# Two GNN layers on one core: receiver's term moved into message and table, deviation in halves, messages two chunks ahead, GpSimd's edge steps unrolled

## Chip and metric

The kernel runs on one core of a Trainium2 chip. The metric is the device time of one execution in microseconds. Median of three runs before the change: 1519.05 us (1518.92 to 1519.62).

## What is computed

x is 50000 nodes by 128 features. There are 25000 edges, sorted by receiver `dst`, each with a sender `src` and 128 attributes. Cut to what matters:

```python
def layer0(h, src, dst):                 # h = relu(layernorm(x))
    m = concat([h[dst], h[src]]) @ W_pre.T + b_pre
    mx, mn, mean, std = segment max, min, mean, sqrt(relu(E[m*m] - mean**2) + 1e-5) over dst
    agg = concat([mx, mn, mean, std])    # zero (std: sqrt(1e-5)) where a node has no edge
    amp = log(max(deg, 1) + 1)
    out = concat([h, agg, agg * amp, agg / amp]) @ W_post.T + b_post
    return out @ W_lin.T + b_lin
x = x + layer0(relu(layernorm(x)), src, dst)
h = relu(layernorm(x))
agg = segment mean of edge_attr over dst
x = x + relu(concat([h, agg]) @ W1 + b1) @ W2 + b2
```

## The kernel before

**Two phases.** The node phase walks over 98 chunks of 512 nodes and computes every node as if it had no edge: layer 0 reduces to a product with the combined weight `comb_x` and a constant, then the second layer norm and MLP, and the result goes to `out`. On its way it writes a table of 256 values a node to HBM: h = layernorm(x) and x. The edge phase walks over 49 chunks of 512 edges, gathers table rows by index (h of the sender into `hs`, h and x of the receiver into `rows`), computes both layers anew for nodes with edges, and scatters the results of each segment's last edge over `out`.

**Order of work.** Each engine runs its own program, written out by hand: `run_passes` calls `node_step(k)` and then `edge_step(k)`, and semaphores (`wait_ge`, `then_inc`) tie the engines together. In `edge_step(k)` an engine works on chunk k, on k+1 ("ahead") and on k-1 ("behind"). A function's first argument is the chunk. Instructions of an engine never overtake each other, nor do the DMAs of a queue in their issue.

**Matrix work of the edge phase** is on TensorE (`pe`). `sender_part` computes the senders' part of the messages of 512 edges by one float32 product; the receiver's term is the same for all edges of a segment and is added after the reduction. `layer0(c, j)` makes tile j of chunk c: for maximum, minimum and mean the value is split in a high and a low float32r half and multiplied in three passes of 384 columns (L607, L608, L611); the deviation is one float32 product (L614); the receiver's h, also split, has three more passes (L617). `hidden` (L699 to L703) and `outputs` are the second layer's MLP.

**VectorE (`dve`)** runs the segmented scans over the messages (`scan_max`, `scan_min`, `scan_sum`, `scan_squares`), the scan over the scaled attributes (`scan_attr`, L1219), `mix` (four tiles a chunk, three instructions each), the low halves (`low_part`), `factors` (L1191, L1193) and `outputs`. **ScalarE (`act`)** evicts, squares, makes the high halves, seeds the accumulators (`seed`), scales the attributes by 1/degree (`scale_attr`, L892) and makes the second layer norm's statistics (`squares`, L814; `spread`, L822) and `normalise`. **GpSimd (`pool`)** issues the indirect DMAs: eight gathers and four scatters a chunk; it copies their indices out of `index` first, and `factor` out of `scale`.

**SyncE (`sp`)** issues the plain DMAs. In `edge_step(k)` it loads five mask rows of chunk k+4 into four buffers, broadcast to 128 partitions, and then the attributes of chunk k+2 into two buffers. The masks' buffers are free when chunk k's scans have read them, so the first mask's DMA waits, among others, for `scan_attr(k)` (the first line quoted stands in the masks' part, where c is k+4):

```python
                        sp.wait_ge(sem("e_attr_run"), c - 3 + EU * i)
                    ...
                c = k + 2
                if edge(c):
                    ...
                        sp.wait_ge(sem("e_turned_attr"), c - 1 + EU * i)
```

The attributes' way is: SyncE's DMA, `scale_attr` on ScalarE, `turn_attr` on TensorE (a transpose into bank 2), `scan_attr` on VectorE.

## Time and profile before

| | us |
|---|---|
| median of three runs | 1519.05 |
| the profiled execution | 1520.14 |
| its span in the trace | 1518.3 |
| TensorE busy | 1445.0 |
| VectorE busy | 1287.0 |
| ScalarE busy | 1142.2 |
| GpSimd busy | 1152.0 |

Times in the trace are microseconds from the span's start. The node phase ends near 550 us, the edge phase's first `layer0` stands near 586 us. Busy time is the union of an engine's instructions; TensorE's instructions overlap each other, so that what one costs is read from start to start, and not from its duration.

### The profile page before, as it was taken

How to read it: one execution, taken by the hardware profiler on the slowest of the kernel's cores; microseconds unless marked ns; L12 is line 12 of the kernel's file. 1: busy time of each engine (PE TensorE's matmuls, PEld its weight loads, DVE VectorE, ACT ScalarE, POOL GpSimd, SP SyncE). 2: the span in 40 equal slices, each digit the busy share in tenths (PEclk: the TensorE clock that was granted, in tenths of full speed). 3: DMA queues.
4: the chain of work that ended last, by engine and by line, in shares of the span. 5: the costliest groups of instructions: out<-in, count | busy, mean ns of one | idle time of the engine just before them, and what ended most of it. 6: DMA issues, size and time to landing. Idle time of an engine off the chain costs nothing.

```text
span 1518.3 us, 34851 instructions
## 1 busy us (share of the span) xinstructions
PE 1445.0 (95%) x8704; PEld 1246.4 (82%) x8704; DVE 1287.0 (85%) x4128; ACT 1142.2 (75%) x2760; POOL 1152.0 (76%) x1427
## 2 busy tenths in 40 slices
PE   2799999999999987999999999999999999999994
PEld 2698998998998976888888888888888888888883
DVE  4899999999999957888888888888888888888881
ACT  1699999999999965777777777777777777777772
POOL 0677777777877876788888888888888888888722
PEclk9699999999999998999999999999999999999997
DMA  3455555555555563343434434333333443444200
GB/s 80 153 204 200 208 200 200 212 198 203 209 196 209 204 228 104 116 116 116 119 111 114 116 113 113 115 114 116 116 115 115 117 117 116 117 119 119 91 16 13
DMA packets 166068, 210.91 MB, mean 139 GB/s; under 512 B 19710, under 2 KB 116217, under 8 KB 166026
## 3 DMA queue, kind: packets, MB, share of 16 engines
q1 hardware_dynamic: 144074, 162.88, 32.7%
q0 software_dynamic: 21952, 47.55, 10.5%
q8 instruction: 17, 0.28, 0.1%
q14 instruction: 25, 0.20, 0.0%
HBM read 123.96 MB, written 90.27 MB: 141 GB/s over the span
## 4 chain that ended last, share of the span: by engine, by line
PE 92%; DVE 2%; issue 2%; DMA 1%; POOL 1%; ACT 1%; SPq 1%; DVEq 0%; POOLq 0%
PE bank L573 12%; PE bank L614 8%; PE bank L617 7%; PE bank L611 7%; PE bank L608 7%; PE bank L607 7%; PE bank L582 6%; PE bank L711 6%; PE bank L699 5%; PE bank L674 3%; PE bank L592 3%; PE bank L594 3%; PE bank L593 3%; PE bank L556 3%; PE bank L564 3%
## 5 line engine op out<-in xcount | busy, mean ns | idle before, releaser
L464 POOL DMA_INDIRECT y<-nout,oidx x196 | 223.3, 1139 | 49.0 <-issue 46.0
L456 POOL DMA_INDIRECT rows<-table,idx x196 | 187.9, 958 | 59.7 <-issue 59.7
L607 PE MATMUL bank<-comb_lo,agg_hi 128*128 128x384 f32 x588 | 221.3, 376 | 0.8 <-ACT bank L885 0.8
L456 POOL DMA_INDIRECT hs<-table,idx x196 | 192.8, 984 | 29.4 <-issue 10.0
L385 POOL TENSOR_TENSOR runs<-nx,b_all 128x512 f32<-128x512 f32 x98 | 125.5, 1281 | 114.6 <-DVE nx L1081 114.6
L573 PE MATMUL bank<-w_sb,nut 128*128 128x128 f32 x1568 | 202.0, 282 | 1.5 <-ACT nut L806 1.5
L573 PEld LDWEIGHTS bank<-w_sb,nut 128*128 128x128 f32 x1568 | 183.9, 193 | 19.8 <-issue 10.0
L611 PE MATMUL bank<-comb_hi,agg_lo 128*128 128x384 f32 x588 | 198.2, 337 | 0.0
L608 PE MATMUL bank<-comb_hi,agg_hi 128*128 128x384 f32 x588 | 198.1, 337 | 0.0
L791 ACT ACTIVATE nh<-nx,nms,nrs 128x128 f32<-128x128 f32 x392 | 161.8, 483 | 1.1 <-DVE nms L1054 0.5
L614 PE MATMUL bank<-comb_sd,agg_sd 128*128 128x384 f32 x392 | 158.1, 485 | 0.0
L397 POOL TENSOR_SCALAR rows<-rows,nmv,nrs 128x128 f32<-128x128 f32 x196 | 153.8, 794 | 0.0
L394 POOL TENSOR_TENSOR xdc<-rows,lone_const 128x512 f32<-128x512 f32 x98 | 124.7, 1272 | 34.4 <-DVE nrs L1091 34.4
L1147 DVE SCALAR_TENSOR_TENSOR part<-bank,factor,rows 128x128 f32<-128x128 f32 x196 | 67.9, 347 | 83.5 <-PE bank L617 83.4
L806 ACT ACTIVATE nut<-bank,b_col 128x512 f32<-128x512 f32 x196 | 126.3, 681 | 6.8 <-PE bank L594 6.6
L885 ACT ACTIVATE bank<-acc_seed 128x384 f32<-128x384 f32 x196 | 96.0, 490 | 43.0 <-DVE nx L1163 38.6
L876 ACT ACTIVATE nut<-bank,b_col 128x512 f32<-128x512 f32 x98 | 66.6, 680 | 79.2 <-PE bank L703 79.2
L617 PE MATMUL bank<-comb_h_lo,hdt 128*128 128x384 f32 x196 | 123.1, 628 | 0.0
L607 PEld LDWEIGHTS bank<-comb_lo,agg_hi 128*128 128x128 f32 x588 | 110.7, 188 | 14.8 <-ACT bank L885 10.7
L608 PEld LDWEIGHTS bank<-comb_hi,agg_hi 128*128 128x128 f32 x588 | 110.8, 188 | 13.5 <-issue 11.5
L611 PEld LDWEIGHTS bank<-comb_hi,agg_lo 128*128 128x128 f32 x588 | 110.5, 188 | 0.2 <-DVE agg_lo L1171 0.2
L582 PE MATMUL bank<-comb_x,hst 128*128 128x128 f32 x784 | 107.6, 282 | 2.8 <-ACT hst L770 2.8
(184 smaller groups left out, 4192.1 us busy)
## 6 DMA issues: line engine op xcount, KB each, us to landing
table<-rows SPq DMA_DIRECT2D x98, 512.0 KB, 2.7
rows<-in_x SPq DMA_DIRECT2D x98, 256.0 KB, 3.1
y<-nout SPq DMA_DIRECT2D x98, 256.0 KB, 2.7
inv<-inv_row SPq DMA_DIRECT2D x49, 256.0 KB, 5.0
keepm<-keepm_row SPq DMA_DIRECT2D x49, 256.0 KB, 5.8
attr<-in_edge_attr SPq DMA_DIRECT2D x48, 256.0 KB
keep<-keep_row SPq DMA_DIRECT2D x49, 128.0 KB, 3.6
reset<-reset_row SPq DMA_DIRECT2D x49, 128.0 KB, 4.6
```

Source lines behind the costliest of these rows:

```text
L397: last = pool.tensor_scalar(nh[:, c % 4, j, :], nx[:, c % 4, j, :], nmv1[:, c % 4, j, 0:1], nrs1[:, c % 4, j:j + 1], ALU.subtract, ALU.mult)
L456: pool.indirect_dma_start(out=to[:, s, j, :], out_offset=None, in_=of, in_offset=bass.IndirectOffsetOnAxis(ap=idx[:, s, which, j:j + 1], a ...
L464: pool.indirect_dma_start(out=out, out_offset=bass.IndirectOffsetOnAxis(ap=oidx[:, c % 4, j:j + 1], axis=0), in_=eout[:, c % 2, j, :], in_ ...
L573: mm = pe.matmul(bank[5][:, j * P:(j + 1) * P], nut[:, c % 2, m, j * P:(j + 1) * P], w2_sb[:, m, :], start=(m == 0), stop=(m == 1))
L582: mm = pe.matmul(bank[1][:, j * P:(j + 1) * P], nht[:, c % 2, j * P:(j + 1) * P], comb_x[:], start=True, stop=True)
L607: pe.matmul(acc[:, 0:SCALERS * P], hi, w_lo, start=False, stop=False, skip_group_check=True)
L608: pe.matmul(acc[:, 0:SCALERS * P], hi, w_hi, start=False, stop=False, skip_group_check=True)
L611: pe.matmul(acc[:, 0:SCALERS * P], lo, w_hi, start=False, stop=False, skip_group_check=True)
L614: pe.matmul(acc[:, 0:SCALERS * P], agg_sd[:, c % 2, cols], comb_sd[:].rearrange("p s f -> p (s f)"), start=False, stop=False, skip_group_c ...
L617: mm = pe.matmul(acc[:, 0:SCALERS * P], h[:, c % 2, cols], w[:].rearrange("p s f -> p (s f)"), start=False, stop=(w is comb_h_hi and h is ...
L791: last = act.activation(nh2[:, b, j, :], nx1[:, b, j, :], ACT.Identity, scale=nrs2[:, b, j:j + 1], bias=nms2[:, b, j:j + 1])
L806: act.activation(nut[:, c % 2, m, :], bank[6 + m][:], ACT.Relu, bias=b1_col[:, m:m + 1]).then_inc(sem("n_ut"), 1)
```

## The change

**Table and message.** `rows` now holds h and x1, x1 being the node's value after the first layer as if it had no edge (the node phase's `nx1`); x itself has a tile of its own, `nx`. The table is written in step k for chunk k, after `n_x1`, where it was chunk k+2. The edge phase starts from x1, and the accumulator's seed leaves out what x1 holds already. The receiver's term goes into the message: `messages` is `sender_part` with a second float32 product of 512 columns (`wd_t`, `hdt`); the three passes with `comb_h_lo` and `comb_h_hi`, and VectorE's `receiver_low`, are gone. **Deviation.** It is split into halves like the other three aggregates, with three float32r passes for one float32 product, a `high_part` on ScalarE and a `low_part` on VectorE. **Order.** Messages are made for chunk k+2 in step k, and all engines' edge steps are put in another order. **GpSimd.** No index copies, its edge steps written out for every chunk, one small operation (`go`) ahead of each four DMAs; `copy_factors` moves to VectorE. SyncE's `edge_step` is as it was.

The diff, cut to its core:

```diff
-    nh, nx = rows[:, :, :, 0:P], rows[:, :, :, P:2 * P]
-    hd, xd = nh, nx
+    nh, nx1 = rows[:, :, :, 0:P], rows[:, :, :, P:2 * P]
+    hd, xd = nh, nx1
+    nx = sb("nx", [P, 4, TILES, P])
...
-                        sp.wait_ge(sem(f"n_tabled{c % 4}"), 16 * (c // 4) + 16 * i)
-                        sp.wait_ge(sem("n_turn1"), c - 3 + NU * i)
+                        sp.wait_ge(sem("n_norm1"), c - 3 + NU * i)
+                        sp.wait_ge(sem("n_norm1_act"), c - 3 + NU * i)
+                        sp.wait_ge(sem("n_norm1_pool"), c - 3 + NU * i)
                         sp.wait_ge(sem("n_xc"), c - 3 + NU * i)
                     sp.dma_start(nx[:, c % 4], node_rows(x, c, i)).then_inc(sem(f"n_in{c % 4}"), 16)
-                c = k + 2
+                c = k
                 if node(c):
 
                     sp.wait_ge(sem("n_norm1"), c + 1 + NU * i)
                     sp.wait_ge(sem("n_norm1_act"), c + 1 + NU * i)
                     sp.wait_ge(sem("n_norm1_pool"), c + 1 + NU * i)
+                    sp.wait_ge(sem("n_x1"), c + 1 + NU * i)
...
+                    pool.wait_ge(sem(f"e_gathered{s}"), 16 * 2 * TILES * (c // 4))
+                    pool.wait_ge(sem("e_turned_s"), c - 3)
+                    pool.wait_ge(sem("e_turned_d"), c - 3)
+                go(0, c, "e_mixed" if c >= 4 else None, TILES * (c - 3))
+                gather_tile(c, 0)
+                gather_tile(c, 1)
+                go(1, c, None, 0)
+                gather_tile(c, 2)
+                gather_tile(c, 3)
...
+                go(2, c, "e_out", c + 1)
                 for j in range(TILES):
-                    if j == 2:
-                        pause(2, c, i)
                     pool.indirect_dma_start(
-                        out=out, out_offset=bass.IndirectOffsetOnAxis(ap=oidx[:, c % 4, j:j + 1], axis=0),
+                        out=out, out_offset=bass.IndirectOffsetOnAxis(ap=column(2, c, j), axis=0),
                         in_=eout[:, c % 2, j, :], in_offset=None,
                         bounds_check=N - 1, oob_is_err=False).then_inc(sem(f"e_scattered{c % 4}"), 16)
...
-                for a in (MX, MN, ME):
+                for a in (MX, MN, ME, SD):
...
-                pe.matmul(acc[:, 0:SCALERS * P], agg_sd[:, c % 2, cols], comb_sd[:].rearrange("p s f -> p (s f)"),
-                          start=False, stop=False, skip_group_check=True)
-                for h, w in ((hdt, comb_h_lo), (hdl, comb_h_hi), (hdt, comb_h_hi)):
-                    mm = pe.matmul(acc[:, 0:SCALERS * P], h[:, c % 2, cols], w[:].rearrange("p s f -> p (s f)"),
-                                   start=False, stop=(w is comb_h_hi and h is hdt), skip_group_check=True)
+                    mm = pe.matmul(acc[:, 0:SCALERS * P], lo, w_hi, start=False, stop=(a == SD), skip_group_check=True)
...
-                pe.matmul(bank[3 + c % 2][:], ws_t[:], hst[:, c % 2, :], start=True, stop=True).then_inc(sem("e_b_psum"), 1)
+                pe.matmul(bank[3 + c % 2][:], ws_t[:], hst[:, c % 2, :], start=True, stop=False)
+                pe.wait_ge(sem("e_hdt"), c + 1 + EU * i)
+                pe.matmul(bank[3 + c % 2][:], wd_t[:], hdt[:, c % 2, :], start=False, stop=True).then_inc(sem("e_b_psum"), 1)
...
-                if ahead:
-                    turn_sender(k + 1, i)
-                    turn_receiver(k + 1, i)
                 if have:
                     turn_attr(k, i)
-                if ahead:
-                    sender_part(k + 1, i)
+                if edge(k + 2):
+                    turn_sender(k + 2, i)
+                    turn_receiver(k + 2, i)
                 if have:
-                    pe.wait_ge(sem("e_hdl"), k + 1 + EU * i)
                     layer0(k, 0, i)
                     layer0(k, 1, i)
+                if edge(k + 2):
+                    messages(k + 2, i)
                 if behind:
-                    turn_normed(k - 1, i, not ahead)
+                    turn_normed(k - 1, i, not edge(k + 2))
...
             def edge_step(k, i):
                 have, ahead, behind = edge(k), edge(k + 1), edge(k - 1)
                 if k == 0:
                     seed(0, 0, i)
                 if ahead:
-                    sender_turned(k + 1, i)
+                    scale_attr(k + 1, i)
+                if behind:
+                    squares(k - 1, i)
                 if have:
                     seed(k, 1, i)
                 if behind:
-                    squares(k - 1, i)
                     spread(k - 1, i)
-                if ahead:
-                    message_squared(k + 1, i)
+                if edge(k + 2):
+                    receiver_turned(k + 2, i)
+                    sender_turned(k + 2, i)
                 if behind:
                     normalise(k - 1, i)
                 if have:
                     seed(k, 2, i)
+                if ahead:
+                    mean_squared(k + 1, i)
                 if behind:
                     normed_turned(k - 1, i)
                 if ahead:
-                    receiver_turned(k + 1, i)
-                    scale_attr(k + 1, i)
                     high_part(ME, "e_mean_b", mean_b[:], k + 1, i)
+                    high_part(MX, "e_max", run_max[:, (k + 1) % 2, :], k + 1, i)
+                    variance_pos(k + 1, i)
+                    high_part(MN, "e_min", run_min[:, (k + 1) % 2, :], k + 1, i)
+                    deviation(k + 1, i)
                 if behind:
                     hidden(0, 7, k - 1, i)
                 if have:
                     seed(k, 3, i)
                 if ahead:
-                    mean_squared(k + 1, i)
+                    high_part(SD, "e_std", var[:], k + 1, i)
                 if behind:
                     out_bias(k - 1, i)
-                if ahead:
-                    high_part(MN, "e_min", run_min[:, (k + 1) % 2, :], k + 1, i)
+                if edge(k + 2):
+                    message_squared(k + 2, i)
                 if behind:
                     hidden(1, 1, k - 1, i)
                 if ahead:
                     if k >= 0:
                         seed(k + 1, 0, i)
-                    variance_pos(k + 1, i)
-                    deviation(k + 1, i)
-                    high_part(MX, "e_max", run_max[:, (k + 1) % 2, :], k + 1, i)
...
@@ -1299,41 +1281,41 @@
 
             def edge_step(k, i):
                 have, ahead, behind = edge(k), edge(k + 1), edge(k - 1)
-                if have:
-                    scan_attr(k, i)
+                if ahead:
+                    scan_max(k + 1, i)
+                    scan_squares(k + 1, i)
+                    scan_sum(k + 1, i)
                 if edge(k - 2):
                     outputs(k - 2, i)
                 if behind:
                     factors(k - 1, i)
+                if ahead:
+                    message_mean(k + 1, i)
                 if have:
                     mix(k, 0, i)
                 if ahead:
-                    scan_sum(k + 1, i)
+                    square_mean(k + 1, i)
                     scan_min(k + 1, i)
-                    message_mean(k + 1, i)
+                    variance(k + 1, i)
                 if behind:
                     normed_low(k - 1, i)
-                if ahead:
-                    receiver_low(k + 1, i)
                 if have:
                     mix(k, 1, i)
                 if ahead:
-                    scan_squares(k + 1, i)
+                    low_part(MX, run_max[:, (k + 1) % 2, :], k + 1, i)
+                if have:
+                    scan_attr(k, i)
+                    mix(k, 2, i)
+                if edge(k + 2):
+                    copy_factors(k + 2, i)
+                if ahead:
+                    low_part(MN, run_min[:, (k + 1) % 2, :], k + 1, i)
                     low_part(ME, mean_b[:], k + 1, i)
-                    square_mean(k + 1, i)
-                if have:
-                    mix(k, 2, i)
-                if ahead:
-                    variance(k + 1, i)
-                    scan_max(k + 1, i)
                 if have:
                     mix(k, 3, i)
-                if ahead:
-                    low_part(MN, run_min[:, (k + 1) % 2, :], k + 1, i)
-                if have:
                     negative_mean(k, i)
                 if ahead:
-                    low_part(MX, run_max[:, (k + 1) % 2, :], k + 1, i)
+                    low_part(SD, var[:], k + 1, i)
 
             run_passes(dve, node_step, edge_step, first_step=-1)
 
```

Three places in the order of instructions. On VectorE, one edge step of the loop around `scan_attr`; before it was the first work of the step (`runs<-keepm` is `scan_attr`, `part` and `nx` are `mix`):

```order
L1219 SCALAR_TENSOR_TENSOR runs<-keepm,runs,bank 128x512 [waits e_u_psum]
L1183 TENSOR_TENSOR nout<-bank,nx 128x512 [waits e_scattered0]
L1191 RECIPROCAL rs<-sd 128x4 [waits e_norm2]
L1193 SCALAR_TENSOR_TENSOR ms<-neg,rs 128x4 [waits e_rs2]
L1147 SCALAR_TENSOR_TENSOR part<-bank,factor,rows 128x128 [waits e_factors,e_gathered0]
L1153 SCALAR_TENSOR_TENSOR part<-bank,factor,part 128x128 [waits e_part]
L1163 SCALAR_TENSOR_TENSOR nx,sum<-bank,part 128x128 [waits e_ms2,e_norm2,e_part2]
L1257 SCALAR_TENSOR_TENSOR runs<-keep,runs,bank 128x512 [waits e_sum,e_mean_b,e_masks_in1,e_bsq]
```

and with the change, from `factors` to `scan_attr` of one step:

```order
L1178 RECIPROCAL rs<-sd 128x4 [waits e_norm2]
L1180 SCALAR_TENSOR_TENSOR ms<-neg,rs 128x4 [waits e_rs2]
L1257 TENSOR_TENSOR mean_b<-runs,inv 128x512 [waits e_mean_b2,e_lo2,e_sum]
L1130 SCALAR_TENSOR_TENSOR part<-bank,factor,rows 128x128 [waits e_factors,e_gathered0]
L1136 SCALAR_TENSOR_TENSOR part<-bank,factor,part 128x128 [waits e_part]
L1150 SCALAR_TENSOR_TENSOR nx,sum<-bank,part 128x128 [waits e_ms2,e_norm2,e_part2]
...
L1228 SCALAR_TENSOR_TENSOR runs<-lift,runs,bank 128x512 [waits e_min,e_lo1,e_masks_in1,e_bsq]
L1270 TENSOR_TENSOR var<-var,mean_b 128x512 [waits e_sq_mean,e_mean_b2]
L1187 SCALAR_TENSOR_TENSOR nh2l<-bank,nh2t 128x512 [waits e_u_psum]
...
L1158 TENSOR_TENSOR agg_lo<-runs,agg_hi 128x512 [waits e_layer0]
L1200 SCALAR_TENSOR_TENSOR runs<-keepm,runs,bank 128x512 [waits e_u_psum]
```

`scan_attr(k)` has moved from ahead of `factors(k-1)` (`rs<-sd`, `ms<-neg,rs`) to behind `factors(k-1)`, two mixes, a scan and five elementwise operations.

On ScalarE, before, the end of one step and the start of the next (`attr<-attr,factor` is `scale_attr`, `sq<-nx,neg` is `squares`, `sd<-sq` is `spread`):

```order
L892 ACTIVATE attr<-attr,factor 128x128 [waits e_factors,e_attr_in0]
L892 ACTIVATE attr<-attr,factor 128x128 x3
...
L885 ACTIVATE bank<-acc_seed 128x384 [waits e_mixed]
L814 ACTIVATE off,sq<-nx,neg 128x128 [waits e_sq2,e_neg2]
L814 ACTIVATE off,sq<-nx,neg 128x128 x3
L822 ACTIVATE sd<-sq,eps_col 128x4 [waits e_rs2,e_sq2]
L852 ACTIVATE bsq<-bank 128x512 [waits e_sqsum,e_b_psum]
```

and with the change, the start of a step:

```order
L863 ACTIVATE attr<-attr,factor 128x128 [waits e_factors,e_attr_in0]
L863 ACTIVATE attr<-attr,factor 128x128 x3
L785 ACTIVATE nx,sq<-nx,neg 128x128 [waits e_sq2,e_neg2]
L785 ACTIVATE nx,sq<-nx,neg 128x128 x3
L856 ACTIVATE bank<-acc_seed 128x384 [waits e_mixed]
L793 ACTIVATE sd<-sq,eps_col 128x4 [waits e_rs2,e_sq2]
```

`scale_attr(k+1)` stood in step k behind `squares(k-1)` and `spread(k-1)`, and now stands ahead of both.

On SyncE, the issues of one step with the change; the list before reads the same but for the line numbers:

```order
L340 DMA keep<-keep_row 128x512 [waits e_sq_mean,e_mean_b,e_attr_run,e_min,e_max]
L340 DMA reset<-reset_row 128x512
L340 DMA lift<-lift_row 128x512
L340 DMA inv<-inv_row 128x512
L340 DMA keepm<-keepm_row 128x512
L352 DMA attr<-in_edge_attr 128x4x128 [waits e_turned_attr]
```

Nothing moved there: the attributes' DMA is queued behind five masks, whose first waits for `e_attr_run`, which `scan_attr` raises.

## Rows read from the trace of the kernel before

**Rows 1.** One stretch: busy PE, PEld, DVE, ACT, POOL; then PEclk, DMA share, GB/s

```profile
800.00:1100.00 300.00, 300.00 (x1620) 253.64 (x1619) 254.02 (x534) 220.65 (x551) 250.26 (x340) 1.00 0.40 115
```

**Rows 2.** Timeline of TensorE over one edge step (start, duration, us)

```profile
844.85 0.81 PE L614 MATMUL bank<-comb_sd,agg_sd 128*128 128x384 f32 x2
...
845.84 0.34 PE L617 MATMUL bank<-comb_h_hi,hdt 128*128 128x384 f32 x1
846.01 0.34 PE L607 MATMUL bank<-comb_lo,agg_hi 128*128 128x384 f32 x1
...
851.94 1.02 PE L699 MATMUL bank<-runs,w_attr 128*128 128x512 f32 x2
...
853.49 1.02 PE L699 MATMUL bank<-runs,w_attr 128*128 128x512 f32 x2
...
863.39 0.81 PE L614 MATMUL bank<-comb_sd,agg_sd 128*128 128x384 f32 x2
```

**Rows 3.** Timeline of VectorE over the same step

```profile
842.68 1.28 DVE L1219 TENSOR_TENSOR_SCAN runs<-keepm,runs,bank 128x512 f32<-128x512 f32 x1 [0.83 <-issue]
...
844.56 0.18 DVE L1191 RECIPROCAL rs<-sd 128x4 f32<-128x4 f32 x1
844.77 0.16 DVE L1193 SCALAR_TENSOR_TENSOR ms<-neg,rs 128x4 f32<-128x4 f32 x1
846.21 0.35 DVE L1147 SCALAR_TENSOR_TENSOR part<-bank,factor,rows 128x128 f32<-128x128 f32 x1 [1.27 <-PE bank L617]
...
847.25 1.28 DVE L1257 TENSOR_TENSOR_SCAN runs<-keep,runs,bank 128x512 f32<-128x512 bf16 x1
848.45 1.25 DVE L1247 TENSOR_TENSOR_SCAN runs<-lift,runs,bank 128x512 f32<-128x512 bf16 x1
849.62 0.67 DVE L1276 TENSOR_TENSOR mean_b<-runs,inv 128x512 f32<-128x512 f32 x1
850.20 0.68 DVE L1206 SCALAR_TENSOR_TENSOR nh2l<-bank,nh2t 128x512 fp32r<-128x512 f32 x1
```

**Rows 4.** Timeline of ScalarE over the same step

```profile
842.15 0.49 ACT L885 ACTIVATE bank<-acc_seed 128x384 f32<-128x384 f32 x1
...
844.23 0.30 ACT L822 ACTIVATE sd<-sq,eps_col 128x4 f32<-128x4 f32 x1
...
850.35 1.27 ACT L892 ACTIVATE attr<-attr,factor 128x128 f32<-128x128 f32 x4
```

**Rows 5.** Timeline of SyncE's DMA issues in the same step

```profile
844.18 0.33 SPq L341 DMA_DIRECT2D keep<-keep_row  x1
...
846.08 0.38 SPq L341 DMA_DIRECT2D keepm<-keepm_row  x1
846.65 0.38 SPq L353 DMA_DIRECT2D attr<-in_edge_attr  x1
```

**Rows 6.** The tile keep, 600 to 1430 us: issue to landing

```profile
DMA to landing us min/median/max: 3.2/3.6/4.2
```

**Rows 7.** The tile keepm, 600 to 1430 us: issue to landing

```profile
DMA to landing us min/median/max: 4.8/5.8/6.4
```

**Rows 8.** GpSimd's DMA groups on the page

```profile
L464 POOL DMA_INDIRECT y<-nout,oidx x196 | 223.3, 1139 | 49.0 <-issue 46.0
L456 POOL DMA_INDIRECT rows<-table,idx x196 | 187.9, 958 | 59.7 <-issue 59.7
...
L456 POOL DMA_INDIRECT hs<-table,idx x196 | 192.8, 984 | 29.4 <-issue 10.0
```

**Rows 9.** Timeline of VectorE, then of GpSimd, near 611 us

```profile
611.30 1.28 DVE L1267 TENSOR_TENSOR_SCAN runs<-keep,runs,bsq 128x512 f32<-128x512 bf16 x1
...
611.67 1.66 POOL L456 DMA_INDIRECT rows<-table,idx  x1 [0.30 <-issue]
```

**Rows 10.** Timelines at the change of phase: GpSimd, then TensorE

```profile
549.56 1.22 POOL L456 DMA_INDIRECT hs<-table,idx  x1 [0.17 <-issue]
...
552.38 0.60 PE L564 MATMUL bank<-ident,nh 128*128 128x128 f32 x4
```

More of the change, by code:

```diff
@@ L236, in run_passes @@
                 edge_step(k - N_HI + 1, 0)
+        if not edge_loop:
+            for k in range(0, E_HI):
+                edge_step(k, 0)
+            return
         for k in range(0, E_LOOP):
@@ L692, in hidden @@
                     pe.wait_ge(sem("e_out"), c + EU * i)
-                if m == 1 and edge(c + 2):
-                    pe.wait_ge(sem("e_hdl"), c + 3 + EU * i)
+                if m == 1 and edge(c + 3):
+                    pe.wait_ge(sem("e_hdt"), c + 4 + EU * i)
                 if c >= 1:
```

202 lines of the change are left out of this document (86 added, 116 removed).

## The prediction, made blind

> **What bounds the kernel now.** I read first the busy time by stretch. Between 800 and 1100 us TensorE is busy for all 300 us at a granted clock of 1.00 (its upper level, 2.4 GHz), while VectorE has 254, GpSimd 250 and ScalarE 221 [rows 1]. So in the edge phase nothing but TensorE's own instructions sets the pace, and every other wait has slack. The period of a chunk is read from one instruction to the same one a step later: the deviation's product of the same tile starts at 844.85 and again at 863.39, so 18.54 us a chunk [rows 2]; 49 chunks make about 908 of the 1518.3 us. The node phase before it is no place where the change moves much: its work a chunk is the same, only the table's write moves by two steps.
>
> **TensorE's part.** From the deviation's product to the next tile's first pass it is 846.01 − 844.85 = 1.16 us a tile: one float32 product and three receiver passes. One float32r pass of 384 columns costs 846.01 − 845.84 = 0.17 [rows 2]. In their place stand three float32r passes, 0.52. That removes 0.64 a tile, 2.56 a chunk. Added is a float32 product of 512 columns. From one such product of the MLP to the next is 853.49 − 851.94 = 1.55, with three float32r products of 512 between; at 0.17 × 512/384 = 0.23 each the float32 one costs 0.86. Net −1.70: TensorE needs **16.84 us a chunk**.
>
> **The other engines.** VectorE loses a low half (`receiver_low`) and gains one (deviation) of 0.58, the step from 849.62 to 850.20 [rows 3], and the factors' copy, taken at 0.2, near the smallest operation there (0.18): about 254/300 × 18.54 = 15.7, and with the small gaps between operations some 16.3. ScalarE: 221/300 × 18.54 = 13.6, and the new high half about as much as a low half, 14.2. GpSimd issues 12 DMAs a chunk: (223.3 + 187.9 + 192.8)/49 = 12.33 [rows 8], with 0.30 of gap ahead of one [rows 9], nine such gaps 2.7. The three `go` are new and no row shows them: at least one small operation (0.18, VectorE's in rows 3, for want of one of GpSimd's), at most a DMA's gap and such an operation, 0.5; I take 0.5 since each waits for semaphores. 12.33 + 2.7 + 1.5 = 16.5. The index copies, 250/300 × 18.54 − 12.33 = 3.1 of today's busy time, go. So all engines together would allow about 17.
>
> **The wait that takes their place.** It is a loop through four engines, one step a turn, and I went round it because the change moves two of its members. Before, `scan_attr(k)` was the step's first work on VectorE; SyncE's first mask DMA followed it by 844.18 − (842.68 + 1.28) = 0.22 [rows 3, 5]; `scale_attr` of the attributes fetched then stood in the middle of ScalarE's next step. A ScalarE instruction at 850.35 [rows 4] used attributes whose DMA had been issued in the previous step; those issued at 846.65 [rows 5], landing near 852 by the estimate below, are used at 850.35 + 18.54 = 868.9. That is 17 us of slack, nearly a step.
>
> After, `scan_attr(k)` stands behind `factors(k-1)`, two mixes and a scan, and `scale_attr(k+2)` is the very first work of ScalarE's step k+1, ahead of `squares(k)` and `spread(k)`, on which `factors(k)` and so `scan_attr(k+1)` depend. The turn of the loop is:
> - scan's end to the first mask's issue: 0.22.
> - to the attributes' landing: their DMA is the sixth in the queue. The fifth, `keepm`, is issued 846.08 − 844.18 = 1.90 after the first [rows 5] and lands 5.8 later in the median [rows 7], so at 7.7; the attributes are issued 0.57 later. Nothing waits for them in the trace of before, so their landing is not shown. I take 7.95, between 7.7 (with `keepm`) and 8.27 (0.57 later), since each mask lands later than the one ahead of it: the first takes 3.6 [rows 6].
> - ScalarE: `scale_attr` 1.27, then `squares` with one seed 844.23 − 842.15 = 2.08, then `spread` 0.30 [rows 4]: 3.65.
> - VectorE: `factors` 844.77 − 844.56 + 0.16 = 0.37; five operations of 0.58 (mean, square mean, variance, `normed_low`, low half), 2.90; two mixes of 847.25 − 846.21 = 1.04, 2.08; `scan_min` 849.62 − 848.45 = 1.17; `scan_attr` 1.28 [rows 3]: 7.80.
>
> Sum 0.22 + 7.95 + 3.65 + 7.80 = **19.6 us a chunk**. This is more than 18.54, and no engine's work lies beside it: while ScalarE waits for the attributes, everything behind in its queue waits too (`squares`, seeds, the receiver's and sender's copies), so TensorE's `layer0` of tile 1 and on waits for seeds, and VectorE's mixes for TensorE. What is late next would be the masks themselves, which have two steps.
>
> Bounds of the unknown landing: the quickest `keepm` (4.8) puts it at 1.90 + 4.8 = 6.7 and the loop at 18.4 (1509); landing as an unloaded mask does, 1.90 + 0.57 + 3.2 [rows 5, 6] = 5.7, puts it at 17.35; the slowest `keepm` plus 0.57, 8.9, at 20.55.
>
> The Trainium skill ("DMA: Bandwidth & Descriptors", section "Queues, rings and completion order") says that a ring's descriptors are consumed in ring order. The rows bear on it: the fifth mask lands 5.8 after its issue and the first 3.6, though the same size [rows 6, 7]; by that rule the attributes land behind `keepm`, as taken above.
>
> **The phase's start and end.** The first messages now need gathers of chunk 2 as well, and the table's last chunk is complete only with the node phase's x1: the first gather, at 549.56 now, comes at about 552, when TensorE turns the last node chunk's normed rows [rows 10], +2.4; partly covered. I take +1.5, between 0 (hidden in the 36 us to the first `layer0`) and 3. In the last three steps no masks are issued ahead of the attributes or no attributes at all: these run at TensorE's 16.84, 3 × (16.84 − 18.54) = −5.1.
>
> **The sum**, against the profiled execution: 1520.1 + 45 × (19.6 − 18.54) + 1.5 − 5.1 = 1564.2. That execution was 1.1 above the median of the runs, so **1563**. In general the time is 1515.4 + 45 × (T − 18.54) with T the period, and it equals 1519 at T = 18.62. The measurement tells about 0.2% (3 us) from no change.
>
> **Rivals.**
> - *TensorE still sets the pace*, and the time falls: T = 16.84 gives 1439. For it: TensorE was at 300 of 300 [rows 1]. Against: the loop, and GpSimd at about the same length. It needs the attributes to land within 16.84 − 11.67 = 5.2 of the scan's end, less than any row gives.
> - *GpSimd sets the pace.* A gather that begins while VectorE runs a scan with two operands in SBUF is stretched until that scan ends: 1.66 instead of its mean 0.958 at 611.67, the scan ending at 611.30 + 1.28 = 612.58 [rows 8, 9]. With DMAs back to back, one or two more in a chunk meet this: 16.5 + about 0.8 = 17.3, time 1460. It decides if the attributes land before 17.3 − 11.67 = 5.6. The Trainium skill ("SBUF — State Buffer", section "Who interferes with whom") says that a VectorE instruction with two SBUF inputs contends with GpSimd's; the trace agrees in these rows.
> - *The loop exists but the DMAs land sooner*, since the queue is less crowded when VectorE is idle: T between 17.35 and 18.6, time 1462 to 1518. For it: the minima in rows 6 and 7. Against: the masks' five broadcasts go together whatever VectorE does, and the median of `keepm` is 1 us over its minimum.
> - *The loop is worse*: the landing of 8.9 gives 20.55 and 1606; and GpSimd's gathers, now packed in fours, share the DMA engines.
>
> **Chances.** Loop over 18.7: 0.71 (its own range 1530 to 1606); loop between 18.55 and 18.7, a time within 3 us: 0.04; loop below: 0.09; GpSimd: 0.09; TensorE: 0.07. Faster thus 0.25, same 0.04, slower 0.71. For 8 in 10 the range runs from 1462, the loop's low bound and just above GpSimd's time, to 1604, near the high bound; outside lie TensorE's and most of GpSimd's case (0.14) and a worse loop (0.05).
>
> **What would show it.** Right: in the edge phase the same product of a tile comes each 19.6 us; TensorE's busy time there falls to some 16.8/19.6 of it, with the idle time before tiles that wait for seeds or mixes; ScalarE sits idle for about 5 us a chunk before `scale_attr`, released by the attributes' DMA; VectorE's `factors` waits for `spread`; SyncE's first mask waits for `scan_attr`. A DMA landing row for the attributes of 5 to 6 us settles the largest term. Wrong, and the time near 1440 to 1460, if the attributes land within 3 us of their issue; then ScalarE's wait is gone and TensorE or GpSimd is busy throughout. Wrong the other way, if a mix or a seed waits for GpSimd's gathers or scatters, which I cost at nothing since rows and factors are gathered two steps ahead.

## The result, and the profile after

The changed kernel took **1657.89 us** in the median of four runs (1650.22 to 1669.53) against 1519.09 for the kernel before beside it: ratio 1.092, 95% interval 1.085 to 1.099. I had forecast 1563 with a range of 1462 to 1604. The direction was right and the loop that I had named is there; but one wait in it was left out, the size was off by 95 us, and the range did not hold the time.

One caution for all that follows: in three groups of runs the kernel before took 1645 to 1772 us, and times from those groups are told apart below and never set against 1519 or 1658.

The page of the profiled execution (1655.76 us) says in its first rows what changed: the span, the busy time of TensorE, and the chain of work that ended last, traced back from the last instruction. TensorE made 92% of that chain before; now it makes 48%.

```profile
span 1653.9 us, 34363 instructions
...
PE 1431.4 (87%) x8403; PEld 1241.9 (75%) x8403; DVE 1291.1 (78%) x4180; ACT 1152.0 (70%) x2812; POOL 1104.8 (67%) x1134
...
PE 48%; DMA 16%; issue 10%; ACT 9%; DVE 8%; SPq 6%; POOL 2%; DVEq 0%; ACTq 0%; POOLq 0%
DMA attr<-in_edge_attr 15%; PE bank L542 11%; SPq L340 6%; PE bank L551 5%; ACT nx L785 4%; PE bank L576 4%; DVE runs L1200 3%; PE bank L636 3%; PE bank L577 3%; PE bank L580 3%; PE bank L561 3%; PE bank L563 3%; PE bank L562 3%; PE bank L525 3%; PE bank L533 3%
```

The same row of the kernel before:

```profile
PE 92%; DVE 2%; issue 2%; DMA 1%; POOL 1%; ACT 1%; SPq 1%; DVEq 0%; POOLq 0%
```

The DMA of the attributes is now the costliest member of the chain, 15% of the span. The busy times by stretch have the columns of [rows 1]. First the node phase of the kernel before, then two stretches of the changed kernel. The node phase is as before, and between 800 and 1100 us no engine is full any more.

```profile
200.00:400.00 200.00, 200.00 (x1477) 180.32 (x1475) 196.54 (x972) 184.85 (x428) 157.65 (x157) 1.00 0.56 203
```

```profile
200.00:400.00 200.00, 200.00 (x1476) 180.74 (x1474) 196.10 (x972) 186.40 (x428) 157.77 (x157) 1.00 0.57 203
800.00:1100.00 300.00, 257.56 (x1285) 220.28 (x1284) 215.66 (x467) 187.10 (x481) 198.43 (x206) 0.89 0.34 99
```

TensorE has 257.6 of 300 at a mean granted clock of 0.89 where it had 300 at 1.00. The cost per chunk is read from one `negative_mean` (`neg<-sum`, near the end of VectorE's step) to the next. The first, the 46th and the last of the changed kernel, and then of the kernel before:

```profile
604.96 0.17 DVE L1280 TENSOR_SCALAR neg<-sum 128x4 f32<-128x4 f32 x1
...
1577.64 0.17 DVE L1280 TENSOR_SCALAR neg<-sum 128x4 f32<-128x4 f32 x1
...
1624.58 0.17 DVE L1280 TENSOR_SCALAR neg<-sum 128x4 f32<-128x4 f32 x1
```

```profile
601.17 0.16 DVE L1298 TENSOR_SCALAR neg<-sum 128x4 f32<-128x4 f32 x1
...
1435.10 0.33 DVE L1298 TENSOR_SCALAR neg<-sum 128x4 f32<-128x4 f32 x1
...
1488.59 0.17 DVE L1298 TENSOR_SCALAR neg<-sum 128x4 f32<-128x4 f32 x1
```

The first 45 periods take 1577.64 − 604.96 = 972.7, **21.6 us a chunk** (18.53 before, 18.54 in [rows 2]); the last three take 46.9 together. The whole difference of the two profiled executions, 135.6 us, is 138.7 in these 45 periods, 3.8 in the start of the phase, −6.5 in the last three chunks and −0.4 in the tail.

**The loop, once round.** The chain of waits, from one `scan_attr` (L1200) to the next (start, duration; a name and a line for each piece):

```profile
1018.70 1.28 DVE runs L1200
1020.20 0.33 SPq L340
1020.62 0.38 SPq L340
1021.10 0.38 SPq L340
1021.66 0.33 SPq L340
1022.09 0.38 SPq L340
1022.65 5.34 DMA attr<-in_edge_attr
1028.10 0.14 ACT attr L863
...
1029.38 1.54 ACT nx L785 x8
1030.91 0.39 ACT bank L856
1031.34 0.44 PE bank L576
...
1034.95 0.30 PE bank L580
1035.26 0.86 PE bank L636 x2
1036.12 0.86 PE bank L638 x2
1036.97 0.45 PE bank L648 x4
1037.53 0.61 ACT nh2t L829
1038.27 0.06 DVE nh2l L1187
...
1040.47 1.28 DVE runs L1200
```

It is the forecast loop: the scan, five masks (L340), the attributes' DMA, `scale_attr` (L863), `squares` (L785). But from there the chain does not go over `spread` and `factors` to VectorE. It goes over `seed(k,1)` (L856) to TensorE: `layer0` of tile 1, twelve passes, then `messages` (L636, L638), `turn_normed` (L648), back to ScalarE (`nh2t`) and only then to VectorE's `normed_low` (L1187). ScalarE's and VectorE's timelines show the same as waits (the bracket is idle time before the row, and who ended it):

```profile
1028.10 1.28 ACT L863 ACTIVATE attr<-attr,factor 128x128 f32<-128x128 f32 x4 [5.00 <-DMA attr<-in_edge_attr]
...
1031.23 0.28 ACT L793 ACTIVATE sd<-sq,eps_col 128x4 f32<-128x4 f32 x1
...
1037.53 0.60 ACT L829 ACTIVATE nh2t<-bank 128x512 fp32r<-128x512 f32 x1 [2.58 <-PE bank L648]
```

```profile
1031.63 0.18 DVE L1178 RECIPROCAL rs<-sd 128x4 f32<-128x4 f32 x1 [2.29 <-ACT sd L793]
...
1038.27 0.69 DVE L1187 SCALAR_TENSOR_TENSOR nh2l<-bank,nh2t 128x512 fp32r<-128x512 f32 x1 [2.26 <-ACT nh2t L829]
```

ScalarE waits 5.00 us for the attributes, as forecast ("about 5 us"). VectorE waits 2.29 for `spread`, as forecast, and then once more, 2.26, for `nh2t`, which was not. The attributes' landing over the phase (issue to landing):

```profile
DMA to landing us min/median/max: 3.9/5.5/6.6
```

Five and a half in the median. With 1.90 + 0.57 = 2.47 from the first mask to the issue of the attributes, that makes 7.97. The turn's terms, mean of the first 42 turns in the trace (each read from rows like those above), beside the forecast:

| term | forecast | measured |
|---|---|---|
| scan's end to first mask | 0.22 | 0.23 |
| to the attributes' landing | 7.95 | 7.97 |
| ScalarE: `scale_attr`, `squares`, seed, `spread` | 3.65 | 3.41 |
| to `factors` | 0 | 0.06 |
| VectorE's own work, `factors` to scan's end | 7.80 | 7.86 |
| VectorE's wait for `nh2t` | 0 | 2.00 |
| turn | 19.6 | 21.5 |

**The wait has three sizes**, and they go with TensorE's clock in tile 1 and in the messages behind it. "Tile 1" is the time from its first pass to the first product of the messages; the 42 turns are those of the table above:

| turns | granted clock in tile 1 | tile 1 | messages | wait for `nh2t` | turn |
|---|---|---|---|---|---|
| 13 | 1.00 | 2.2 | 1.7 | 0.59 to 0.73, mean 0.65 | 20.2 |
| 17 | 0.54 to 0.76 | 2.8 to 3.8 | 1.7 to 2.8 | 1.81 to 2.35, mean 2.11 | 21.5 |
| 12 | 0.50 | 4.0 | 2.3 to 2.8 | 2.68 to 3.48, mean 3.27 | 23.1 |

The turn shown above is one of the 17. TensorE had stood idle for 3.02 us before tile 1, and most of its passes then follow each other at 0.32 instead of 0.17. Two windows, one in the work ahead of the idle time and one over tile 1, show the granted clock (the third number from the end):

```profile
1026.00:1028.00 2.00, 2.00 (x15) 2.00 (x12) 2.00 (x3) 0.00 (x0) 1.70 (x2) 1.00 0.66 213
1031.40:1035.00 3.60, 3.60 (x12) 3.60 (x13) 3.26 (x9) 3.55 (x9) 2.99 (x3) 0.54 0.31 91
```

The clock is 1.00 in the first, its upper level of 2.4 GHz. The mean of 0.54 in the second says that nearly all of it ran at the lower level of 1.2 GHz. Twelve passes that need 2.1 us took 3.7. In another turn TensorE came out of 3.16 us of idle time at the upper level; TensorE's timeline, and VectorE's behind it:

```profile
790.67 0.44 PE L576 MATMUL bank<-comb_lo,agg_hi 128*128 128x384 f32 x1 [3.16 <-ACT bank L856]
790.95 0.33 PE L577 MATMUL bank<-comb_hi,agg_hi 128*128 128x384 f32 x1
...
792.68 0.34 PE L580 MATMUL bank<-comb_hi,agg_lo 128*128 128x384 f32 x1
792.85 1.02 PE L636 MATMUL bank<-hst,ws_t 128*128 128x512 f32 x2
```

```profile
795.91 0.69 DVE L1187 SCALAR_TENSOR_TENSOR nh2l<-bank,nh2t 128x512 fp32r<-128x512 f32 x1 [0.67 <-ACT nh2t L829]
```

The tile takes 792.85 − 790.67 = 2.18, and VectorE waits 0.67. The idle time before tile 1 does not tell which it will be: it was 2.60 to 3.56 us before the 13 tiles at 1.00, and 2.34 to 5.91 before the other 29. The Trainium skill ("TensorE: Matmul & The Clock Gate", section "HAM oscillation — how this bites in real kernels") describes a kernel in which every DMA wait lowers the clock for the work behind it; the trace agrees for 29 of these 42 turns and not for the other 13, though every one of them has the wait for the attributes' DMA in it.

### The profile page after: what moved, and what is told of

It reads as the page before. It is cut to its first block, busy times and chain, and to the rows that moved or that the text cites. A ratio compares the mean times of both kernels' runs of the same rounds, so it can differ in the third digit from the quotient of the medians.

```text
span 1653.9 us, 34363 instructions
## 1 busy us (share of the span) xinstructions
PE 1431.4 (87%) x8403; PEld 1241.9 (75%) x8403; DVE 1291.1 (78%) x4180; ACT 1152.0 (70%) x2812; POOL 1104.8 (67%) x1134
## 4 chain that ended last, share of the span: by engine, by line
PE 48%; DMA 16%; issue 10%; ACT 9%; DVE 8%; SPq 6%; POOL 2%; DVEq 0%; ACTq 0%; POOLq 0%
DMA attr<-in_edge_attr 15%; PE bank L542 11%; SPq L340 6%; PE bank L551 5%; ACT nx L785 4%; PE bank L576 4%; DVE runs L1200 3%; PE bank L636 3%; PE bank L577 3%; PE bank L580 3%; PE bank L561 3%; PE bank L563 3%; PE bank L562 3%; PE bank L525 3%; PE bank L533 3%
## 5 line engine op out<-in xcount | busy, mean ns | idle before, releaser
L580 PE MATMUL bank<-comb_hi,agg_lo 128*128 128x384 f32 x784 | 284.2, 362 | 0.0
L577 PE MATMUL bank<-comb_hi,agg_hi 128*128 128x384 f32 x784 | 284.0, 362 | 0.0
L417 POOL DMA_INDIRECT rows<-table,index x196 | 242.8, 1239 | 60.8 <-issue 60.8
L451 POOL DMA_INDIRECT y<-nout,index x196 | 211.4, 1079 | 54.5 <-issue 54.3
L417 POOL DMA_INDIRECT hs<-table,index x196 | 199.7, 1019 | 45.2 <-issue 38.3
L863 ACT ACTIVATE attr<-attr,factor 128x128 f32<-128x128 f32 x196 | 62.6, 390 | 231.8 <-DMA attr<-in_edge_attr 231.8
L384 POOL TENSOR_TENSOR runs<-rows,b_all 128x512 f32<-128x512 f32 x98 | 126.0, 1285 | 113.0 <-DVE rows L1057 113.0
L755 ACT ACTIVATE nh<-rows,nms,nrs 128x128 f32<-128x128 f32 x392 | 161.8, 483 | 0.9 <-DVE nms L1030 0.3
L400 POOL TENSOR_SCALAR rows<-nx,nmv,nrs 128x128 f32<-128x128 f32 x196 | 154.6, 798 | 0.0
L397 POOL TENSOR_TENSOR xdc<-nx,lone_const 128x512 f32<-128x512 f32 x98 | 124.9, 1274 | 35.2 <-DVE nrs L1067 35.1
L1187 DVE SCALAR_TENSOR_TENSOR nh2l<-bank,nh2t 128x512 fp32r<-128x512 f32 x49 | 33.9, 691 | 97.8 <-ACT nh2t L829 97.8
L663 PE MATMUL bank<-runs,w_attr 128*128 128x512 f32 x196 | 101.9, 602 | 0.7 <-issue 0.7
```

The lines of the kernel that those rows point to most:

```text
L384: pool.tensor_tensor(nx1b[:, c % 4], nx1[:, c % 4], b2_all[:], ALU.add).then_inc(sem("n_x1b"), 1)
L397: pool.tensor_tensor(nxc[:, c % 2], nx[:, c % 4], lone_const[:], ALU.add).then_inc(sem("n_xc"), 1)
L400: last = pool.tensor_scalar(nh[:, c % 4, j, :], nx[:, c % 4, j, :], nmv1[:, c % 4, j, 0:1], nrs1[:, c % 4, j:j + 1], ALU.subtract, ALU.mult)
L417: pool.indirect_dma_start(out=to[:, s, j, :], out_offset=None, in_=of, in_offset=bass.IndirectOffsetOnAxis(ap=column(which, c, j), axis=0) ...
L451: pool.indirect_dma_start(out=out, out_offset=bass.IndirectOffsetOnAxis(ap=column(2, c, j), axis=0), in_=eout[:, c % 2, j, :], in_offset=None,
L577: pe.matmul(acc[:, 0:SCALERS * P], hi, w_hi, start=False, stop=False, skip_group_check=True)
```

## Experiments

### The attributes ahead of the masks

SyncE issues `attr(k+2)` before the masks of chunk k+4; its own wait (`turn_attr(k)`) is met early. The rest is the changed kernel.

```diff
             def edge_step(k, i):
+                c = k + 2
+                if edge(c):
+                    ...
+                        sp.dma_start(attr[:, s], ...)
                 c = k + 4
                 if edge(c):
                     ...
-                c = k + 2
-                ...
```

> The changed kernel with SyncE's attributes ahead of the masks, a third time, as the yardstick beside the two runs below. Theory: 2% below the kernel before on this chip, undisturbed chunks 16.4 to 17.8, stalls in the others.

Measured: **1459.21 us** (1456.80 to 1466.25), the kernel before 1519.06 beside it, ratio 0.962 (0.960 to 0.965). ScalarE no longer waits for the attributes at all. The loop alone had turned a gain of 60 us into a loss of 139. Of the first 45 periods 25 are 16.7 and 17 are 17.6 to 18.6; the mean is 17.2. What bounds it now is between TensorE and GpSimd. The stretch has the columns of [rows 1]; below it stand GpSimd's groups on the page:

```profile
800.00:1100.00 300.00, 293.56 (x1636) 252.27 (x1635) 273.18 (x594) 244.00 (x607) 243.16 (x264) 1.00 0.43 124
```

```profile
L417 POOL DMA_INDIRECT hs<-table,index x196 | 222.7, 1136 | 45.2 <-issue 42.1
L451 POOL DMA_INDIRECT y<-nout,index x196 | 212.3, 1083 | 54.5 <-issue 51.9
L417 POOL DMA_INDIRECT rows<-table,index x196 | 205.3, 1047 | 59.7 <-issue 59.7
```

GpSimd's DMAs cost (222.7 + 212.3 + 205.3)/49 = 13.07 a chunk instead of the 12.33 taken from [rows 8]; 85 of them follow each other from 849 to 970 us with at most 0.7 us between the end of one and the start of the next. This is the rival "GpSimd sets the pace", forecast at 17.3 and 1460; the two runs that follow bear on it.

### Fewer scatters

The same with three of a chunk's four scatters left out: those rows of the output are not written. The waits for the scatters count one a chunk instead of four.

```diff
-                for j in range(TILES):
+                for j in range(1):
                     pool.indirect_dma_start(
                         out=out, ...
```

> The kernel of attr_ahead with three of a chunk's four scatters left out, so that GpSimd issues 9 DMAs a chunk and rests some 4 us in each. Theory: the stalls come with GpSimd's unbroken series of DMAs (24 in a row, the stall in the last third), so they are gone: chunks of 16.4 to 17.4 throughout, time 1430 to 1470 on any chip. Rival: the stalls are the chip's or the other engines' own and stay: within 40 us of attr_ahead.

Measured: **1432.54 us** (1430.25 to 1435.37), ratio 0.943 (0.941 to 0.945), beside the 1459 above.

```profile
800.00:1100.00 300.00, 300.00 (x1691) 260.08 (x1690) 280.87 (x613) 250.72 (x630) 204.67 (x216) 1.00 0.41 121
```

TensorE is full, every period of the loop but the first is 16.7 (forecast 16.84), and GpSimd is busy for 205 of 300 us. So the three scatters cost 1459 − 1433 = 27 us of the version with the loop cut. The stalls that the expectation speaks of are told of below; attr_ahead had none of them beside this run, so the run can't say what ends them.

### GpSimd's program as before

The kernel of attr_ahead with the old `edge_step` of GpSimd: in a loop, with index copies and a small operation behind each two DMAs (the old `gather_rows_of`, `scatter_rows_of`, `go`, `pause`, `gather`, `scatter`; `copy_factors` stays on VectorE).

```diff
...
+                pool.tensor_copy(idx[:, s].rearrange("p w (r h) -> p w r h", h=2), index[:, 0:2, t, :]).then_inc(sem("e_idx"), 1)
...
+                    if j % 2 == 1:
+                        pause(j // 2, c, i)
...
-            run_passes(pool, node_step, edge_step, edge_loop=False)
+            run_passes(pool, node_step, edge_step)
```

> The kernel of attr_ahead with GpSimd's edge steps as before the change (in a loop, index copies, a small operation after each two DMAs). Theory: with its small operations GpSimd needs about 17.5 us a chunk and is as unbroken as before, so that the stalls stay as in attr_ahead, within 40 us of it. Rival, it is the unrolled GpSimd program or its missing pauses that stall the others: the stalls go, 1460 to 1500.

Measured: **1506.24 us** (1503.64 to 1511.22), ratio 0.991 (0.989 to 0.993). Neither expectation holds: it is 47 us over attr_ahead and 6 over the rival's range, at 16.7 to 22.9 a chunk. TensorE now waits for gathers that land late; the row of the table of waits between 660 and 1380 us that names them (us in total, times, longest):

```profile
PE bank L622 <- DMA rows<-table,idx: 45.6, 28, 3.4
```

So the new GpSimd program is worth 47 us once the loop is cut; which part of it, the unrolling, the missing small operations or the place of the waits, is not told apart.

### scale_attr back in the middle of ScalarE's step

```diff
-                if ahead:
-                    scale_attr(k + 1, i)
                 if behind:
                     squares(k - 1, i)
...
                     normed_turned(k - 1, i)
                 if ahead:
+                    scale_attr(k + 1, i)
                     high_part(ME, "e_mean_b", mean_b[:], k + 1, i)
```

> scale_attr(k+1) behind normed_turned(k-1) on ScalarE, SyncE as in the changed kernel. Theory: where the kernel before takes 1519 the loop is cut as in attr_ahead (1459) and GpSimd sets the pace: period 17.1 to 17.5, time 1455 to 1475. Rival: stalls of this order's own, as in the three runs where the kernel before took over 1640: over 1490 here too.

Measured: **1466.30 us** (1463.91 to 1468.34), the kernel before 1518.50, ratio 0.966 (0.964 to 0.967); of the first 45 periods all but the first are 17.3 to 17.5. Moving one call on ScalarE is enough to take away the whole loss. Nothing waits for the attributes' DMA, with SyncE's queue as it was. The period is GpSimd's: from 729 to 1387 us its 455 DMAs follow each other with at most 0.7 us between them, and twelve take 17.34 from start to start.

### turn_normed ahead of messages on TensorE

```diff
-                if edge(k + 2):
-                    messages(k + 2, i)
                 if behind:
                     turn_normed(k - 1, i, not edge(k + 2))
+                if edge(k + 2):
+                    messages(k + 2, i)
```

> turn_normed(k-1) ahead of messages(k+2) on TensorE, else the changed kernel. Theory: where the kernel before takes 1519, VectorE's wait for nh2t falls from 2.0 to under 0.4 us a chunk, the period from 21.5 to 19.6 to 19.9, the time from 1658 to 1575 to 1590. Rival: the time stays within 20 us of 1658 as another wait takes the place.

Measured: **1584.63 us** (1583.69 to 1585.86), the kernel before 1519.27, ratio 1.043 (1.041 to 1.045). The loop stays, its branch over TensorE gets shorter by the messages' 1.7 us. VectorE's wait for `nh2t` is 0.15 in the mean of the first 42 turns and zero in 27 of them; here one that has it:

```profile
1016.74 0.69 DVE L1187 SCALAR_TENSOR_TENSOR nh2l<-bank,nh2t 128x512 fp32r<-128x512 f32 x1 [0.54 <-ACT nh2t L829]
```

The mean turn in the trace is 20.0 (19.6 to 19.9 expected): the attributes land 8.31 after the first mask's issue here, instead of 7.97. This is very nearly the forecast's own loop, without the branch that it left out, and the time is 22 us over the forecast's 1563.

### Place in the queue or the wait

The attributes ahead of the masks, but still held until `scan_attr(k)`:

```diff
+                        sp.wait_ge(sem("e_turned_attr"), c - 1 + EU * i)
+                        sp.wait_ge(sem("e_attr_run"), c - 1 + EU * i)
+                    ...
+                        sp.dma_start(attr[:, s], ...)
                 c = k + 4
```

> The changed kernel with SyncE's DMA of the attributes of chunk k+2 ahead of the five masks' DMAs of chunk k+4 instead of behind them, still held until scan_attr(k) is done. It tells place in the queue from the wait. Theory: the loop holds, but 4.4 us of its 7.9 us from the scan's end to the landing are the queue; alone the attributes land in about 3.5 us as the first mask does; the period falls to about 17.1 or to what another engine allows, the time to 1450 to 1475. Rival, the transfer itself takes the 5.5 us from issue to landing that it shows now: only 2.5 us are saved, the period is 19.0 to 19.3 and the time 1540 to 1560.

> Attributes ahead of the masks in SyncE's queue but still held until scan_attr(k), where the kernel before takes 1519. Theory: the queue is 4.4 of the 7.9 us to the landing; period 17.1 to 17.5, time 1460 to 1480. Rival, the transfer itself takes 5.5 us: 19.0 to 19.3, 1540 to 1560.

Both runs fell where the kernel before took 1764 and 1772 us, so the times decide nothing on the forecast periods (1688.81, ratio 0.960, 0.952 to 0.968; 1681.10, ratio 0.944, 0.933 to 0.954; the changed kernel beside the second took 1710). The trace of the first shows one issue and the ScalarE instruction that waited for its landing:

```profile
752.95 0.38 SPq L335 DMA_DIRECT2D attr<-in_edge_attr  x1
...
755.92 1.28 ACT L864 ACTIVATE attr<-attr,factor 128x128 f32<-128x128 f32 x4 [0.54 <-DMA attr<-in_edge_attr]
```

It is 2.97 us from issue to use, where it takes 5.5 behind five masks. In the 26 turns of this trace in which ScalarE waited for the landing it is 2.5 to 3.0, in the 27 of the second 2.7 to 3.5. With the 2.47 of the five issues, 5.0 of the 8.0 us from the first mask's issue to the landing are the place behind the masks. That the period would fall to 17.1 is not shown.

### The same variants where the kernel before took 1645 to 1772 us

Three groups of runs, told apart by the second column. The first two were made before the runs above that have 1519 beside them, the third between those and the last two (scale_mid_d, turn_first_d). `after_again` is the changed kernel unaltered; the first group has no run of it:

| kernel | the kernel before beside it | time | ratio (95%) |
|---|---|---|---|
| turn_first | 1764 | 1655 | 0.939 (0.933 to 0.945) |
| scale_mid | 1764 | 1742 | none given |
| attr_ahead | 1764 | 1690 | 0.951 (0.942 to 0.960) |
| after_again | 1645 | 1697 | 1.037 (1.028 to 1.047) |
| turn_first_b | 1645 | 1654 | 1.006 (1.001 to 1.012) |
| scale_mid_b | 1645 | 1706 | 1.041 (1.032 to 1.050) |
| attr_ahead_b | 1645 | 1603 | 0.980 (0.971 to 0.990) |
| turn_first_c | 1772 | 1663 | 0.941 (0.933 to 0.948) |
| scale_mid_c | 1772 | 1755 | 0.989 (0.979 to 1.000) |
| after_again_c | 1772 | 1710 | 0.969 (0.963 to 0.976) |

> The changed kernel with one swap on TensorE: turn_normed(k-1) ahead of messages(k+2). Theory: the turn of the loop (attributes' DMA, scale_attr, squares, factors, scan_attr) has a side branch that I left out, seed(k,1), layer0(k,1) at the lower clock, messages(k+2), turn_normed, nh2t, normed_low, and it is this branch that VectorE waits for, 2.3 us a chunk. Without the messages' 1.7 us in it the period falls from 21.5 to about 19.8 and the time from 1658 by about 46 x 1.7 to 1575 to 1590. Rival: the branch is late because of something ahead of layer0 tile 1 alone, and the order behind it doesn't matter: 1640 to 1658.

> The changed kernel with scale_attr(k+1) on ScalarE moved from the front of the step to behind normed_turned(k-1), about where it was before the change. Theory: the DMA's latency lies beside ScalarE's work again, the loop is cut, TensorE or GpSimd sets the pace: period 16.9 to 17.4, time 1445 to 1470, no idle time of ScalarE ahead of scale_attr. Rival: the attributes are late for this place too, or other waits of the new order bound it: period 18 or more, time over 1495.

> The changed kernel with SyncE's DMA of the attributes of chunk k+2 ahead of the masks' and with only its own wait (turn_attr(k)), which is met at the start of TensorE's step k. Theory: the loop is cut at SyncE; the attributes have more than half a step to land; the period is that of TensorE or GpSimd, 16.9 to 17.4, time 1445 to 1470, the same as with scale_attr moved. Rival: if the place of scale_attr at the front of the step hurts by itself (it delays squares and factors by 1.3 us), this is slower than the kernel with scale_attr moved by 5 us or more.

> The changed kernel unaltered, beside the same variants on one chip. On the chip of the last four runs the kernel before took 1764 us instead of 1519, with waits that end at no instruction of the trace, so that those four can't be set against 1658. Theory: ratio to the kernel before 1.09 where that takes 1519; near 0.95 to 1.0 on a chip where it takes 1764. All comparisons of the variants are made with this run.

The b and c runs had much the same expectations. For turn_first_b it was 70 to 80 us below the changed kernel beside it, and for after_again_c a ratio of 1.09. Both missed. Against the changed kernel of its own group turn_first is 42 and 47 us lower, attr_ahead_b 94 lower, and scale_mid 9 and 45 higher. From these groups alone one would say that moving `scale_attr` does not help. The traces say otherwise: in scale_mid_b chunks of 16.7 to 17.8 alternate with chunks of 20 to 32, and in the long ones engines stand idle with all their inputs done. TensorE's timeline has the receiver's transposes, and ScalarE's the copy (L807) that waits for them and for nothing newer:

```profile
881.37 0.60 PE L615 MATMUL bank<-ident,rows 128*128 128x128 f32 x4
...
882.22 0.28 ACT L793 ACTIVATE sd<-sq,eps_col 128x4 f32<-128x4 f32 x1
890.33 0.60 ACT L807 ACTIVATE hdt<-bank 128x512 f32<-128x512 f32 x1 [7.83 <-remote]
```

The transposes end at 882.0 and ScalarE starts at 890.33, after 7.83 us that the profile puts down to no instruction of this core. I then supposed that GpSimd's unbroken series of DMAs (24 in a row, the stall in the last third) caused them, and expected that for the run with fewer scatters. An unbroken series alone does not do it: attr_ahead_c has 85 in a row and scale_mid_d 455, neither has such a stall, and in the group of attr_ahead_c the kernel before, run once more unaltered, has none either:

> The kernel before, for its trace on this chip: two chips have timed it at 1764 and 1645 us where the trace that I read had 1519. Theory: its edge phase has the same sort of stall as the variants with the loop cut (engines that stand idle for 3 to 12 us with every input done, late in a long unbroken series of GpSimd's DMAs), 120 to 245 us in all, and its undisturbed chunks still take 18.5. Rival: everything is uniformly slower, by a lower clock.

Measured: 1519.06 us (1517.41 to 1521.22), ratio 1.000, periods of 18.5 and 18.6 in all but the first and last of the edge phase. Neither the theory nor the rival could show, since the kernel before took 1519 here; no trace of it was taken where it took 1645 us or more. The group at 1645 and this one ran on the same chip, so it is not the chip alone; what makes the difference is open. In the traces of the slower groups the node phase is as in the others up to 540 us, and all that is longer stands behind it.

## Why the prediction missed

**What bounds before: right.** TensorE alone at 18.54.

**TensorE's new price: right.** 16.84 forecast, 16.7 measured where nothing else bounds (cut_few_scatters).

**GpSimd: the base too low, the rival right in its number.** 16.5 was the sum; the rival with stretched gathers said 17.3 and 1460; the kernel with the loop cut has 17.2 and 1459 (17.3 and 1466 in scale_mid_d). The DMAs rose from 12.33 to 13.07 a chunk. Its reason, gathers stretched by scans, holds in part. Between 620 and 1400 us 68 of 532 DMAs last over 1.4 us in attr_ahead_c, where it was 5 of 504 before; but only 18 of the 68 lie beside a scan, the others beside mixes, `normed_low` and other elementwise work of VectorE. The row that the rival was read from says less than was read: that gather ended at 611.67 + 1.66 = 613.33, which is 0.75 after the scan's end and not with it.

**The loop: found, and each term that was in its sum sized within 0.25 us.** scale_mid_d and attr_ahead_c, which each cut it at another place, both take its whole price away (192 and 199 us off 1658). The landing rested on a comparison that is not clean: the prediction calls `keep` and `keepm` the same size, and they are not. The page of the kernel before has (KB of one transfer, median us to landing)

```profile
keepm<-keepm_row SPq DMA_DIRECT2D x49, 256.0 KB, 5.8
...
keep<-keep_row SPq DMA_DIRECT2D x49, 128.0 KB, 3.6
```

so that 5.8 against 3.6 us mixes place in the queue and size. The attributes, one transfer of one size, show the place by itself: 2.9 us in the median at the head of the queue, 5.5 behind the masks. The order was as taken: in all 23 turns whose trace has both landings the attributes land 0.7 to 1.6 us behind `keepm`.

**The step that failed** is the sentence that "ScalarE: `scale_attr` 1.27, then `squares` with one seed ... then `spread`" leads to VectorE, whose work then follows without a wait. The term for VectorE, 7.80, sums its instructions from `factors` to `scan_attr`; `normed_low` stands in it with its 0.58 and no wait, and the prediction gives no reason for that. The wait measured 2.00 us a turn. But the seed among ScalarE's instructions is that of tile 1. It is late by the same landing, so `layer0` of tile 1, `messages` and `turn_normed` follow in TensorE's order, and `normed_low` waits for what they end with, by way of ScalarE's `nh2t`. The prediction names the late seeds ("TensorE's `layer0` of tile 1 and on waits for seeds") and does not go on along that row. With TensorE at its upper level the branch from tile 1's first pass to `normed_low` takes 795.91 − 790.67 = 5.24 in the rows above, of which `layer0` and `messages` stood priced in the prediction, and VectorE then waits 0.67. The 13 turns of this kind take 20.2 in the mean. By the prediction's formula that alone is 1515.4 + 45 × (20.2 − 18.54) = 1590, inside the range.

**The larger part of it is the clock.** The other 1.35 us of the mean 2.00 come with TensorE at 1.2 GHz behind its idle time: tile 1 takes 3.5 to 4.0 us instead of 2.2 in most of those 29 turns, and the messages 2.3 to 2.8 instead of 1.7 in the 12 longest. The forecast priced the loop at full clock although it said itself that TensorE would stand idle. turn_first_d, in which the branch is 1.7 shorter and the wait nearly gone, gave 73 us back. It shows that the wait sets the period; the two shares, 0.65 and 1.35, are read from the turns of one trace, and no run holds the clock up by itself.

**In numbers**: 45 × (21.6 − 19.6) = 90 of the 95 us; the start (3.8 forecast at 1.5) and the last three chunks (−6.5 for −5.1) make 1; most of the rest is that the profiled execution lies 2.1 under the median of its runs here, where before it lay 1.1 above.

**The range** was built on the landing, which came out at the value taken, and on engines without the loop. Its upper end was the slowest landing in a loop of fixed other terms; a term that is left out was nowhere in it.

## What to carry to other kernels

When a transfer's trigger moves later in one engine's step and its first user moves earlier in another's, follow the dependence once round through every engine before trusting that work per engine; here two moves of a few lines each made a loop through SyncE, DMA, ScalarE, TensorE and VectorE that cost 139 us instead of a gain of 60. Go round such a loop by all branches: whatever stands behind the late instruction on its engine is late too, on the engines it feeds as well. Price TensorE's part behind an idle stretch at the lower clock as well as at the upper, and let the range hold both.

## What was not expected of the hardware

Nearly the same idle time of TensorE (3.02 and 3.16 us) was followed by 0.54 of the clock in one turn and by 1.00 in another, so that one loop has turns of 19.5 and of 23.7 us, and four runs of it spread from 1650 to 1670 where four of the kernel before lie within 0.7. The attributes' transfer, 256 KB, takes 2.5 to 3.5 us at the head of the queue and 5.5 in the median behind five masks. Of GpSimd's indirect DMAs in the new order, 68 of 532 last over 1.4 us (attr_ahead_c), where it was 5 of 504 before. And the kernel before took 1645 us in one group of runs and 1519 in a later one on the same chip, and 1764 and 1772 on two others; the variants' traces from the slower groups have stalls in the edge phase at whose end the profile sees no instruction of the core, the longest of 17 us (ScalarE in scale_mid).
